# Four graph layers on one core: transfers of 125 rows issued as 112 and 13 rows, degrees in halves, weight sums earlier

## The chip, the core and the metric

The kernel runs on one core of a Trainium2 chip. The metric is the device time of one execution in microseconds: the median of the runs shown, beside the lowest and the highest. The core has five engines with instruction queues of their own, which wait for one another by semaphores: PE (matrix products, with PEld loading its weights), DVE (vector), ACT (scalar and table functions), POOL and SP. Here SP, ACT and POOL issue DMA transfers; 16 DMA engines move the data. The profile also names the clock that the throttle granted to PE: 1.00 is 2.4 GHz and 0.50 is 1.2 GHz.

## What is computed

x has 1250 nodes of 512 features, and 21250 directed edges (src, dst), own loops among them. Four graph layers follow one another, each as x = layernorm(x + layer(x)):

```
L0: h = x @ W_gat (8 heads of 64); alpha = softmax over the edges into a node of
    leaky_relu(a_src[src] + a_dst[dst]); out = sum of alpha * h[src]; batch norm, gelu, + x @ W_skip
L1: x0, x1 = linear(x); tpw = small network of 3 silu layers on edge_attr_8; per edge products of
    tpw, x[src] and edge_attr_4, summed by dst; linear; / 10
L2: s, t = (h @ W) @ a; att = softmax over the edges of leaky_relu(s[row] + t[col]);
    agg = sum of att * h[col]; out = silu(agg) @ base_w.T + sum over 8 B-splines basis(agg) @ spline_w
L3: neighbor_mean = sum over edges of x[src] / max(deg, 1); relu([x, neighbor_mean] @ w.T)
```

## The kernel before

Nodes lie as NB = 10 blocks of NP = 125 rows; edge lists lie as 125 rows of 170 edges. HB = 5 blocks are a half, KT = 4 blocks of 128 features make 512. Each engine's program is written out by hand, with its own order and constant semaphore counts; a DMA adds 16 to its semaphore when it has landed. The stages run in this order.

- **Start.** SP loads dst, src, edge_attr_4, edge_attr_8 and the second half of x (L539 to L543; 83, 83, 332, 664 and 1250 KB), ACT the first half of x and w_gat (L1420, L1421; 1250 and 1024 KB). DVE waits for dst (L1845) and sorts edges by destination; its first result (L1855) opens PE's stream: two small products, ten x_blocks of transposes (L838; the second half of x is awaited at L834), five gat_blocks (L845), then count_order (L819), which also needs DVE's second result (L1911). POOL scatters the sorted edge records to HBM (L717).
- **Counts and layer 0.** Edges become a 1250 x 1250 matrix of counts: cd (a view of cnt_d) and its transpose cnt_s. The edge network of layer 1 runs beside DVE's maxima; PE then waits for DVE at L1030. Eight attention heads follow.
- **Layer 1.** PE's linear_up makes xup; ACT copies each block to one of two buffers (L1663; from the third block on, it awaits the store of the block two before), SP stores it (L619), and POOL gathers the rows by edge after all ten (L774, L775).
- **Layer 2, attention.** In two halves: DVE makes row maxima (half_terms), PE and ACT spread them (half_rows), DVE makes tiles (half_tiles: t_tile L2067, ACT's exponential, p_tile L2071), PE multiplies x by them (L1261). DVE then adds the tiles (add_tile, L2294), reduces the degrees deg from cd (L2314), and waits for PE's column sums (L1271). rden2 = 1 / sums (L2319, L2322) scales feature blocks 0, 1, 2 of aggT (L2325), while PE still multiplies block 3 (L1290).
- **Spline stage.** 36 steps g (two halves of SUBS = 18): a function of aggT (silu for the first two steps of a half) from ACT and DVE, products with weight parts on PE (L1309 pairs, L1319 single). weight_sums(g) forms four sums of the loaded weight parts (L2331 to L2334; the first three are called at L2393, after the scaling), node_sums(g) four sums of the function's blocks (L2344 to L2347), which PE awaits. SP stores the counts to HBM (L641, 3052 KB) once rden2 is begun.
- **Layer 3.** PE makes z = x @ w_near (L1374); ACT copies the high part and stores it (L1802), DVE makes the low part and SP stores it (L668). POOL gathers a few rows of z after all twenty stores (L796 to L798), ACT copies them to big_z (L1829), and PE's gathered_part (L1400) uses them after near_part of block 0 (L1394) and self_part (L1384). SP stores the ten blocks of the output (L672) and waits for all.

Of the kernel before, what the change touches and what calls it, by code (L numbers as in the profile page):

```python
# [10 lines left out]
NP, NB = 125, 10  # L11
# [82 lines left out]
def build(nc, a, out):  # L94
# [8 lines left out]
    with ctx:  # L103
# [427 lines left out]

        def bass_row(v, p):
            return v.rearrange("(a n) -> a n", a=1).to_broadcast([p, v.shape[0]])
# [3 lines left out]
        def _(sp):  # L537

            sp.dma_start(dsti, a["dst"].rearrange("(p e) -> p e", p=NP)).then_inc(s_dst_in, 16)  # L539
            sp.dma_start(srci, a["src"].rearrange("(p e) -> p e", p=NP)).then_inc(s_rec_in, 16)  # L540
            sp.dma_start(a4, a["edge_attr_4"].rearrange("(p e) k -> p e k", p=NP)).then_inc(s_rec_in, 16)
            sp.dma_start(a8, a["edge_attr_8"].rearrange("(p e) k -> p e k", p=NP)).then_inc(s_rec_in, 16)
            sp.dma_start(x_sb[:, HB:, :], a["x"].rearrange("(b p) n -> p b n", p=NP)[:, HB:, :]).then_inc(s_x_in1, 16)  # L543
# [97 lines left out]
            sp.dma_start(cnt_rows.rearrange("(b p) n -> p b n", p=NP), cnt_s[:]).then_inc(s_cntrow_out, 16)  # L641
# [24 lines left out]
            for b in range(NB):  # L666
                sp.wait_ge(s_zlo_ok, b + 1)
                sp.dma_start(z_rows[N + b * NP:N + (b + 1) * NP, :], z_lo[:NP, b, :].bitcast(f32)).then_inc(s_zrow_out, 16)  # L668

            for b in range(NB):  # L670
                sp.wait_ge(s_x_ok, 3 * NB + b + 1)
                sp.dma_start(out[b * NP:(b + 1) * NP, :], x_sb[:, b, :]).then_inc(s_out_done, 16)  # L672
            sp.wait_ge(s_out_done, 16 * NB)
# [3 lines left out]
        def _(pool):  # L677
# [86 lines left out]
            def gathers(i, par, tiles):  # L764
# [8 lines left out]
                if par == 0:  # L773
                    pool.wait_ge(s_xup_out0, 16 * NB // 2)  # L774
                    pool.wait_ge(s_xup_out1, 16 * NB // 2)  # L775
# [16 lines left out]
            pool.wait_ge(s_cntrow_out, 16)  # L792
# [3 lines left out]
            pool.wait_ge(s_zrow_out, 16 * 2 * NB)  # L796
# [6 lines left out]
        def _(pe):  # L803
# [28 lines left out]
            def x_block(b):  # L832
                if b % HB == 0:
                    pe.wait_ge(s_x_in if b == 0 else s_x_in1, 16)  # L834
# [582 lines left out]
        def _(act):  # L1417
            A = nc.scalar.activation

            act.dma_start(x_sb[:, 0:HB, :], a["x"].rearrange("(b p) n -> p b n", p=NP)[:, 0:HB, :]).then_inc(s_x_in, 16)  # L1420
# [238 lines left out]
            def xup_out(b):  # L1659
                act.wait_ge(s_xup_ps, b + 1)  # L1660
                if b >= 2:
                    act.wait_ge(s_xup_out0 if b % 2 == 0 else s_xup_out1, 16 * (b // 2))
# [862 lines left out]
```

## Time and profile before

| | us |
|---|---|
| median of 3 runs (lowest, highest) | 1581.47 (1580.15, 1582.06) |
| profiled execution | 1582.99 |
| its span, first to last instruction | 1581.5 |
| busy in it: PE, DVE, ACT, POOL | 1373.6, 1354.2, 903.0, 480.1 |
| chain that ended last: PE, DVE, issue, ACT, DMA | 51%, 24%, 12%, 5%, 5% |
| mean granted clock of PE | 0.951 |

The chain is followed back from the last instruction, at each step to what released it. "issue" is time in which an engine waited for nothing that the profile shows. The DMA share is the mean busy share of the 16 DMA engines. In a row of the timeline the brackets hold the engine's idle time just before and what ended it.

### The profile page before, as it was taken

What the parts mean: (1) busy time and instruction counts of PE and PEld (TensorE: products, weight loads), DVE (VectorE), ACT (ScalarE), POOL (GpSimd) and SP (SyncE); (2) the same over time, 40 slices, a digit from 0 to 9 for tenths busy, and PEclk for the clock granted to TensorE, in tenths of its full rate; (3) what the DMA queues carried; (4) which work ended last, traced back from release to release, by engine and by line L of the source; (5) the groups of instructions that cost most, each with busy time, mean ns of one, the idle gap of its engine ahead of it and who ended that gap; (6) DMA issues with size and microseconds to landing.
All of it is one profiled execution on the core that took longest, in us unless ns stands there. A gap on an engine that the chain in (4) does not pass through costs nothing.

```text
span 1581.5 us, 25111 instructions
## 1 busy us (share of the span) xinstructions
PE 1373.6 (87%) x8237; PEld 885.5 (56%) x8237; DVE 1354.2 (86%) x2065; ACT 903.0 (57%) x1949; POOL 480.1 (30%) x488
## 2 busy tenths in 40 slices
PE   1978898837688887789999999979999999999997
PEld 1555444602333333566666666756667777776465
DVE  8875999899899999759999999777989979996244
ACT  1286555628565565558888888543168849772300
POOL 1788888840000100236666666200000000000000
PEclk9998999859899999689999999989999999999998
DMA  4201000126111210246666766400144444342301
GB/s 128 69 6 9 6 7 7 14 70 192 53 58 48 60 52 17 77 133 212 198 201 193 214 197 196 76 1 1 54 132 135 134 145 170 136 143 69 117 24 43
DMA packets 76686, 150.26 MB, mean 95 GB/s; under 512 B 13722, under 2 KB 32268, under 8 KB 76477
## 3 DMA queue, kind: packets, MB, share of 16 engines
q1 hardware_dynamic: 50531, 83.18, 16.1%
q0 software_dynamic: 23328, 59.50, 15.0%
q10 hardware_dynamic: 2746, 6.59, 1.3%
q8 instruction: 38, 0.62, 0.2%
q14 instruction: 43, 0.35, 0.1%
HBM read 116.13 MB, written 32.91 MB: 94 GB/s over the span
## 4 chain that ended last, share of the span: by engine, by line
PE 51%; DVE 24%; issue 12%; ACT 5%; DMA 5%; DVEq 2%; POOL 0%; SPq 0%; POOLq 0%; ACTq 0%
PE PS L1309 14%; DVE arena L2071 7%; DVE arena L2037 5%; PE PS L1167 5%; PE PS L1261 4%; PE PS L1319 4%; DVE arena L2067 3%; PE PS L931 3%; PE PS L1394 3%; PE PS L1153 3%; DVE arena L2233 3%; ACT arena L1456 2%; PE PS L845 2%; DMA x_sb<-in_x 2%; PE PS L1374 2%
## 5 line engine op out<-in xcount | busy, mean ns | idle before, releaser
L717 POOL DMA_INDIRECT recs<-arena x170 | 239.3, 1408 | 89.4 <-issue 88.8
L1079 PE MATMUL PS<-arena 125*128 125x512 f32 (+1 forms) x480 | 190.1, 533 | 43.4 <-DVE arena L2071 43.3
L781 POOL DMA_INDIRECT arena<-xup,gidx x205 | 194.8, 950 | 104.7 <-issue 52.4
L1167 PEld LDWEIGHTS PS<-arena 128*32 128x32 f32 x3280 | 174.1, 109 | 88.3 <-ACT arena L1694 81.9
L1694 ACT ACTIVATE arena<-arena,gslot 128x32 f32<-128x32 f32 x820 | 186.3, 309 | 55.2 <-PE PS L1167 48.0
L1167 PE MATMUL PS<-arena 128*32 128x128 f32 (+1 forms) x3280 | 201.9, 306 | 6.2 <-DVE arena L2225 3.9
L2225 DVE TENSOR_TENSOR arena<-PS,arena 128x1536 f32<-128x1536 f32 (+1 forms) x103 | 179.0, 1738 | 0.0
L1079 PEld LDWEIGHTS PS<-arena 125*128 125x128 f32 x480 | 85.6, 191 | 147.8 <-issue 77.6
L1626 ACT ACTIVATE arena<-arena,c 125x1250 f32<-125x1250 f32 x80 | 106.7, 1336 | 97.6 <-DVE arena L2067 97.6
L2067 DVE SCALAR_TENSOR_TENSOR arena<-arena,c 125x1250 f32<-125x1250 f32 (+1 forms) x100 | 137.7, 1380 | 14.0 <-ACT arena L1748 12.9
L1309 PE MATMUL PS<-arena,cnt_d 128*125 128x256 f32 x576 | 148.4, 380 | 0.0
L794 POOL DMA_INDIRECT cnt_d<-cnt_rows,bidx_c x1 | 0.9, 946 | 463.8 <-DVE bvalid L2453 463.8
L1309 PE MATMUL PS<-arena 128*125 128x256 f32 x432 | 118.1, 383 | 3.6 <-DVE cnt_d L2347 3.5
L1309 PEld LDWEIGHTS PS<-arena,cnt_d 128*125 128x125 f32 x576 | 108.7, 189 | 16.4
L1153 PE MATMUL PS<-arena 64*128 64x512 f32 x410 | 117.5, 649 | 0.0
L2071 DVE SCALAR_TENSOR_TENSOR arena<-arena,cnt_s 125x1250 f32<-125x1250 f32 x80 | 116.0, 1450 | 0.0
L1512 ACT ACTIVATE arena<-PS 125x626 uint16<-125x626 f32 x102 | 69.2, 692 | 60.1 <-PE PS L931 60.0
L1309 PEld LDWEIGHTS PS<-arena 128*125 128x125 f32 x432 | 81.6, 189 | 30.7 <-issue 20.2
L2221 DVE TENSOR_TENSOR arena<-PS,arena 128x512 f32<-128x512 f32 (+1 forms) x103 | 70.9, 688 | 19.4 <-DMA arena<-xup,gidx 14.8
L931 PE MATMUL PS<-arena 128*125 128x512 bf16 (+1 forms) x408 | 73.1, 311 | 15.8 <-DVE arena L1992 15.4
L2233 DVE TENSOR_TENSOR arena<-PS,arena 128x256 f32 x205 | 84.8, 414 | 1.3 <-PE PS L1167 0.5
L931 PEld LDWEIGHTS PS<-arena 128*125 128x125 bf16 x408 | 44.6, 142 | 63.7 <-DVE arena L1992 38.9
(395 smaller groups left out, 2536.2 us busy)
## 6 DMA issues: line engine op xcount, KB each, us to landing
arena<-in_spline_wT SPq DMA_DIRECT2D x32, 512.0 KB, 4.1
t_rows<-arena SPq DMA_DIRECT2D x18, 512.0 KB, 5.1
arena<-t_rows SPq DMA_DIRECT2D x18, 512.0 KB, 4.5
arena<-uv_rows SPq DMA_DIRECT2D x14, 610.4 KB
arena<-h_rows SPq DMA_DIRECT2D x26, 256.0 KB
h_rows<-arena SPq DMA_DIRECT2D x24, 256.0 KB, 2.8
arena<-xup,gidx POOLq DMA_INDIRECT x205, 3.7
cnt_rows<-cnt_s SPq DMA_DIRECT2D x1, 3051.8 KB
```

Of the source, the lines that this page charges most:

```text
L717: pool.indirect_dma_start(out=recs, out_offset=bass.IndirectOffsetOnAxis(pos[:, c:c + 1], 0), in_=rec[:, c, :], in_offset=None).then_inc(s ...
L781: pool.indirect_dma_start(out=ring[:, m, :], out_offset=None, in_=xup, in_offset=bass.IndirectOffsetOnAxis(gidx[:, par, m:m + 1], 0))\
L931: ins = t.matmul(PS[:NP, 2 * (n % 3) + q, 0:n1 - n0], oh_dst[:, n % (2 * WP), :, e], oh_src[:, 2 * (n % WP) + e, n0:n1], start=(e == 0), s ...
L1079: ins = t.matmul(PS[:, 3 * par + q, 0:n1 - n0], hs[:, sblk, par * C:par * C + 2 * C], wt[:, sblk % WR, n0:n1], start=(sblk == 0), stop=(sb ...
L1153: t.matmul(PS[:, tpw_bank[(2 * k + q) % 4], :], h3[r, buf, k * 128:(k + 1) * 128], w_m4[r, :], start=True, stop=True, tile_position=(q * H ...
L1167: ins = t.matmul(PS[quad * DB:(quad + 1) * DB, bank, o0 * MUL:o0 * MUL + w], sel4[:, s, v * DB:(v + 1) * DB], prod[:, s, c0 * MUL:c1 * MUL ...
L1309: ins = t.matmul(PS[:NP, bank, c * HD:(c + 1) * HD], lhs, w_part(g, w), start=(s == 0 and m in ((0, 1, 3, 6) if j == 0 else (0, 1, 3))), s ...
L1694: ins = A(sel4[:, s, y * DB:(y + 1) * DB], eq4[:, m // 4, s * DB:(s + 1) * DB], ACT.Copy, scale=gslot[:, par, c + R_Y + y:c + R_Y + y + 1])
L2067: v.scalar_tensor_tensor(dst, U, cc, V, ALU.add, ALU.max).then_inc(ok, 1)
L2071: v.scalar_tensor_tensor(dst, e, 1.0, cm, ALU.min, ALU.mult).then_inc(ok, 1)
L2225: v.tensor_tensor(pr[:, :, :, 1:4, :], w[:, :, :, 1, :].unsqueeze(3).to_broadcast([128, n, 2, 3, MUL]), xg[:, :, 1:4, :].unsqueeze(2).to_b ...
L2233: v.tensor_tensor(d, PS[:, 2 + m % 4, 0:256], d, ALU.add).then_inc(s_gsum_ok, 1)
```

## The change

Every transfer to or from 125 rows that SP and ACT issue, except recs, weights and rows of other shapes, is issued as two: rows 0 to 111 and rows 112 to 124. These are dst, src, both edge attributes and both halves of x, the xup blocks, the counts, the high and low z rows, and the output blocks. Their semaphore counts double. DVE's degree reduction is done by halves of five blocks: the first before the tiles of the first half of layer 2, the second where the whole was. The first three weight_sums move from behind the scaling of aggT to before the wait for the column sums. The scaling goes through blocks 0, 2, 1, and ACT's first silu, which uses blocks 0 and 2, waits for two blocks instead of three.

```
+        ROWS = (slice(0, NP // 16 * 16), slice(NP // 16 * 16, NP))
...
-            sp.dma_start(x_sb[:, HB:, :], a["x"].rearrange("(b p) n -> p b n", p=NP)[:, HB:, :]).then_inc(s_x_in1, 16)
+            for dst_tile, view, done in (
+                    (dsti, a["dst"].rearrange("(p e) -> p e", p=NP), s_dst_in),
...
+                    (x_sb[:, HB:, :], x_rows[:, HB:, :], s_x_in1)):
+                for r in ROWS:
+                    sp.dma_start(dst_tile[r], view[r]).then_inc(done, 16)
...
-                sp.dma_start(xup[b * NP:(b + 1) * NP, :], xup_st[:, b % 2, :]).then_inc(s_xup_out0 if b % 2 == 0 else s_xup_out1, 16)
+                for r in ROWS:
+                    sp.dma_start(xup[b * NP:(b + 1) * NP, :][r], xup_st[r, b % 2, :])\
+                      .then_inc(s_xup_out0 if b % 2 == 0 else s_xup_out1, 16)
...
-            sp.dma_start(cnt_rows.rearrange("(b p) n -> p b n", p=NP), cnt_s[:]).then_inc(s_cntrow_out, 16)
+            for r in ROWS:
+                sp.dma_start(cnt_rows.rearrange("(b p) n -> p b n", p=NP)[r], cnt_s[r]).then_inc(s_cntrow_out, 16)
...
+                for r in ROWS:
+                    sp.dma_start(z_rows[N + b * NP:N + (b + 1) * NP, :][r], z_lo[r, b, :].bitcast(f32)).then_inc(s_zrow_out, 16)
...
+                for r in ROWS:
+                    sp.dma_start(out[b * NP:(b + 1) * NP, :][r], x_sb[r, b, :]).then_inc(s_out_done, 16)
+            sp.wait_ge(s_out_done, 32 * NB)
...
+            for r in ROWS:
+                act.dma_start(x_sb[r, 0:HB, :], a["x"].rearrange("(b p) n -> p b n", p=NP)[r, 0:HB, :]).then_inc(s_x_in, 16)
...
-                    act.wait_ge(s_aggT_ok, KT + 1 if h else KT - 1 + s)
+                    act.wait_ge(s_aggT_ok, KT + 1 if h else KT if s else KT - 2)
...
+                for r in ROWS:
+                    act.dma_start(z_rows[b * NP:(b + 1) * NP, :][r], z_hi[r, b, :].bitcast(f32)).then_inc(s_zrow_out, 16)
...
+            def degrees(hf):
+                bs = slice(hf * HB, (hf + 1) * HB)
+                link(v.tensor_reduce(deg[:, bs], cd[:, bs, :], X, ALU.add))
+            degrees(0)
             half_tiles(0)
             half_terms(1)
             half_tiles(1)
             for j in range(1, NB):
                 add_tile(j)
-            link(v.tensor_reduce(deg[:], cd, X, ALU.add))
+            degrees(1)
...
+            for g in range(3):
+                weight_sums(g)
+
             dve.wait_ge(s_l2_agg, 3)
...
-            for f in range(KT - 1):
+            for f in (0, 2, 1):
                 dve.wait_ge(s_l2_cp, f + KT)
...
-            for g in range(3):
-                weight_sums(g)
             node_sums(0)
```

## Rows read from the trace of the kernel before

**Rows 1.** Stretches: busy us of each engine; granted clock, DMA share, GB/s.

```profile
14.00:27.00 13.00, 0.00 (x0) 0.00 (x0) 12.97 (x4) 0.00 (x0) 0.00 (x0) 1.00 0.32 128
38.00:44.00 6.00, 6.00 (x23) 4.51 (x24) 5.69 (x11) 2.95 (x5) 0.00 (x0) 1.00 0.87 294
```

**Rows 2.** Timeline of PE (start, us, engine, line, operation; idle before and its releaser).

```profile
38.00 4.64 PE L838 MATMUL PS<-ident,x_sb 125*128 125x125 f32 x20 [5.40 <-DMA x_sb<-in_x]
60.30 0.29 PE L819 MATMUL PS<-arena,upper 125*125 125x20 f32 x2
```

**Rows 3.** Timeline of POOL and DVE before the first PE work.

```profile
4.65 2.39 POOL L698 IOTA iota<- 128x416 f16 x1
5.45 1.69 DVE L1846 TENSOR_SCALAR arena<-arena 125x170 int32<-125x170 int32 x1 [3.03 <-DMA arena<-in_dst]
56.59 0.18 DVE L1911 TENSOR_TENSOR arena<-arena 125x19 f32<-125x19 f16 x1
```

**Rows 4.** Timeline of PE at the end of the small network.

```profile
400.72 4.56 PE L1030 MATMUL PS<-ident,uv 125*125 125x125 f32 x20 [8.54 <-DVEq L2057]
```

**Rows 5.** Chain (start, us, what) at xup; the page's DMA issues.

```profile
684.58 4.00 DMA xup<-arena
689.29 4.10 DMA xup<-arena
h_rows<-arena SPq DMA_DIRECT2D x24, 256.0 KB, 2.8
arena<-in_L_gnn_W_up SPq DMA_DIRECT2D x2, 64.0 KB, 1.9
```

**Rows 6.** Timeline of DVE and PE in layer 2, attention.

```profile
1062.29 1.65 DVE L2067 SCALAR_TENSOR_TENSOR arena<-arena,c 125x625 f32<-125x625 f32 x2 [2.87 <-ACT arena L1748]
1065.00 7.36 PE L1261 MATMUL PS<-arena,x_sb 125*128 125x512 f32 x14 [3.41 <-DVE arena L2071]
1125.11 13.17 DVE L2314 TENSOR_REDUCE deg<-cnt_d 125x10 f32<-125x12500 uint16 x1
1139.64 1.46 DVE L2319 TENSOR_SCALAR arena<-PS 128x1250 f32<-128x1250 f32 x1 [1.15 <-PE PS L1271]
```

**Rows 7.** Timeline, chain and one stretch at the start of the spline stage.

```profile
1139.36 16.97 PE L1290 MATMUL PS<-arena,x_sb 125*128 125x512 f32 x48
1149.13 4.20 DVE L2325 TENSOR_TENSOR arena<-arena 128x1250 f32<-128x1250 f32 x3
1157.67 0.42 DVE L2334 TENSOR_TENSOR arena<-arena 128x256 f32<-128x256 f32 x1
1159.81 1.88 PE L1309 MATMUL PS<-arena 128*125 128x256 f32 x4 [3.48 <-DVE cnt_d L2347]
...
1159.81 7.97 PE PS L1309 x28
1169.49 6.04 PE PS L1309 x28
1161.00:1162.00 1.00, 1.00 (x4) 0.76 (x3) 0.41 (x2) 1.00 (x2) 0.00 (x0) 0.50 0.97 322
```

**Rows 8.** Timeline of SP and PE, and the chain, at the z rows.

```profile
1464.12 24.64 SPq L668 DMA_DIRECT2D z_rows<-z_lo  x10
1484.25 14.90 DMA z_rows<-z_lo
1504.07 0.47 PE L1400 MATMUL PS<-big_z,big_cnt 128*125 128x512 f32 x1 [2.84 <-ACT big_z L1829]
1504.53 6.21 PE PS L1394 x20
1514.41 4.67 PE PS L1394 x20
```

**Rows 9.** Timeline of SP and its waits (us, times, longest), end.

```profile
1574.43 0.92 SPq L672 DMA_DIRECT2D out<-x_sb  x2
SPq L103 <- DMA out<-x_sb: 5.7, 1, 5.7
```

More of the change, by code:

```diff
@@ L537, in _ @@
         def _(sp):
[L539 to L542, printed above, removed]
-            sp.dma_start(x_sb[:, HB:, :], a["x"].rearrange("(b p) n -> p b n", p=NP)[:, HB:, :]).then_inc(s_x_in1, 16)
+            x_rows = a["x"].rearrange("(b p) n -> p b n", p=NP)
+            for dst_tile, view, done in (
+                    (dsti, a["dst"].rearrange("(p e) -> p e", p=NP), s_dst_in),
+                    (srci, a["src"].rearrange("(p e) -> p e", p=NP), s_rec_in),
+                    (a4, a["edge_attr_4"].rearrange("(p e) k -> p e k", p=NP), s_rec_in),
+                    (a8, a["edge_attr_8"].rearrange("(p e) k -> p e k", p=NP), s_rec_in),
+                    (x_sb[:, HB:, :], x_rows[:, HB:, :], s_x_in1)):
+                for r in ROWS:
+                    sp.dma_start(dst_tile[r], view[r]).then_inc(done, 16)
             sp.wait_ge(s_wdiag_zero, 1)
@@ L773, in gathers @@
                 if par == 0:
-                    pool.wait_ge(s_xup_out0, 16 * NB // 2)
-                    pool.wait_ge(s_xup_out1, 16 * NB // 2)
+                    pool.wait_ge(s_xup_out0, 32 * NB // 2)
+                    pool.wait_ge(s_xup_out1, 32 * NB // 2)
                 pool.nop(nofuse=True)
@@ L791, in _ @@
             pool.wait_ge(s_big_ok, 3)
-            pool.wait_ge(s_cntrow_out, 16)
+            pool.wait_ge(s_cntrow_out, 32)
             pool.nop(nofuse=True)
@@ L795, in _ @@
                                     in_offset=bass.IndirectOffsetOnAxis(bidx_c[:, 0:1], 0)).then_inc(s_bigrow_in, 16)
-            pool.wait_ge(s_zrow_out, 16 * 2 * NB)
+            pool.wait_ge(s_zrow_out, 32 * 2 * NB)
             pool.nop(nofuse=True)
@@ L833, in x_block @@
                 if b % HB == 0:
-                    pe.wait_ge(s_x_in if b == 0 else s_x_in1, 16)
+                    pe.wait_ge(s_x_in if b == 0 else s_x_in1, 32)
                 if b >= 2:
@@ L1661, in xup_out @@
                 if b >= 2:
-                    act.wait_ge(s_xup_out0 if b % 2 == 0 else s_xup_out1, 16 * (b // 2))
+                    act.wait_ge(s_xup_out0 if b % 2 == 0 else s_xup_out1, 32 * (b // 2))
                 A(xup_st[:, b % 2, :], PS[:NP, 2 + b % 2, :], ACT.Copy, scale=float(MUL) ** -0.5).then_inc(s_xup_cp, 1)
@@ L1801, in store_high @@
                 act.wait_ge(s_z_cp, b + 1)
-                act.dma_start(z_rows[b * NP:(b + 1) * NP, :], z_hi[:NP, b, :].bitcast(f32)).then_inc(s_zrow_out, 16)
+                for r in ROWS:
+                    act.dma_start(z_rows[b * NP:(b + 1) * NP, :][r], z_hi[r, b, :].bitcast(f32)).then_inc(s_zrow_out, 16)
             def x3_in(b):
@@ L1844, in _ @@
             v.memset(blk, 0.0)
-            dve.wait_ge(s_dst_in, 16)
+            dve.wait_ge(s_dst_in, 32)
             v.tensor_scalar(blk_i, dsti, DB.bit_length() - 1, None, ALU.arith_shift_right)
@@ L1855, in _ @@
             v.tensor_tensor(tot_e[:, 1:NDB], cum_e[:, 1:NDB, EC - 1], cum_e[:, 0:NDB - 1, EC - 1], ALU.subtract).then_inc(s_tot_ok, 1)
-            dve.wait_ge(s_rec_in, 48)
+            dve.wait_ge(s_rec_in, 96)
             v.tensor_scalar(rec[:, :, R_DL], dl_i, -1.0, None, ALU.mult)
@@ L2334, in weight_sums @@
                 v.tensor_tensor(t4, b21, t2w, ALU.subtract)
+            for g in range(3):
+                weight_sums(g)
+            dve.wait_ge(s_l2_agg, 3)
+            ins = v.tensor_scalar(rden2, PS[:, 0:3, :].rearrange("p a n -> p (a n)")[:, 0:N], 0.5, None, ALU.max)
+            ins.then_inc(s_psum_ok, 1)
+            dve.wait_ge(s_psum_ok, NB)
+            link(v.reciprocal(rden2, rden2))
+            for f in (0, 2, 1):
+                dve.wait_ge(s_l2_cp, f + KT)
+                v.tensor_tensor(aggT[:, f, :], aggT[:, f, :], rden2, ALU.mult).then_inc(s_aggT_ok, 1)
             def node_sums(g):
```

11 lines of the change are left out of this document (removed).

## The prediction

> **What bounds the kernel now.** I read the chain of work that ended last first, then the waits, then the timeline around each wait that a changed transfer or a moved step touches, and the table of stretches for the clock and the DMA share. The reader is to see that no single resource bounds the kernel: the stages follow one another, and a gain counts only where a wait of the chain's engine ends on what is changed. Four such waits are on transfers of 125 rows, and one is on DVE's order.
>
> The transfers themselves come first. In the stretch in which only 125-row loads run, the DMA share is 0.32 at 128 GB/s, which is 5 engines of 16; where 128-row transfers run it is 0.87 at 294 GB/s [rows 1]. So a 125-row transfer uses 5 engines. That 112 rows use 16 is likely from the 128-row rows, but no row shows 112 rows or 13.
>
> **Start (3.7 us gained).** PE transposes the first half of x, idles 5.40 us until the second half lands, and goes on at 38.00; it reaches the count products (L819) at 60.30 [rows 2]. DVE has what they need at 56.59 + 0.18 = 56.77 [rows 3], 3.53 us before. On 16 engines (294 GB/s, so 16 us for the 4.8 MB of all first loads) the second half is there long before 32.6, PE's idle time goes, and PE is 5.4 us early; but L819 then waits for DVE. So this place gives 3.53 us, plus what DVE itself gains. DVE starts at 5.45 when dst lands, 4.4 us after its issue. Its pieces should land at 3.4 (1.9 us, the 64 KB load [rows 5], after a second issue near 1.5) to 4.4. But L1846 lasts 1.69 us for 170 elements a partition, where L2314 reduces 12,500 in 13.17 [rows 6], 0.18 us for 170; and it ends just after POOL's iota, which ends at 4.65 + 2.39 = 7.04 [rows 3]. DVE was held by POOL, and an earlier dst would bring one or two short instructions ahead of that hold, not the rest. I take 0.2 us of the 2.0 possible: 3.7 in all, between 3.3 and 5.5. The Trainium skill, SBUF — State Buffer, "Who interferes with whom", says that DVE's two-port modes and a GpSimd instruction lock each other out for a whole instruction. The row agrees; without such a lock the whole kernel would come 1.2 us lower, at 1565.6.
>
> From L819 on everything hangs on DVE, PE and ACT in turn, so the 3.7 us travel. The one thing that doesn't move with them is POOL's scatter of records, which feeds the small network; that network ends early and PE then waits 8.54 us for DVE [rows 4], so it may fall behind by the 3.7 us.
>
> **xup rows (2.1 us gained).** A store takes 4.00 us, ACT refills the buffer, and the last store takes 4.10, after which POOL may gather [rows 5]. A 256 KB store from 128 rows lands in 2.8 us [rows 5]. The second piece is issued some 0.4 us after the first (two issues of SP take 0.92 us [rows 9]) and has little data; I take 3.0 us for a pair, between 2.8 and 3.6. That is 1.0 + 1.1 = 2.1 us, between 0.9 and 2.5.
>
> **Degrees, first half (3.8 us lost).** The reduction takes 13.17 us over ten blocks, so 6.6 for five. It is put before the tiles of the first half, where DVE idles only 2.87 us, from 1059.42 to 1062.29 [rows 6]. It ends near 1066.1, so the first tile is 3.8 us late, and PE waits for it already now (3.41 us before L1261 [rows 6]). Behind the tiles queue ACT's exponentials and PE's products. A block has twelve product entries of 7.36 / 14 = 0.53 us and only two DVE steps of 0.83 [rows 6], so DVE catches up and PE doesn't: 3.8 us, at most 4.2. If PE's clock rises sooner after the later restart, up to 1.9 us comes back (what a restart loses at rows 7).
>
> **Degrees, second half, and weight sums (hidden).** Now the reduction runs from 1125.11 to 1138.3, and DVE waits 1.15 us for PE's column sums [rows 6]. In its place come 6.6 us and the twelve weight sums, from the end of L2325 at 1153.3 to 1158.1, 4.8 us [rows 7]. They end near 1136.7, 2.9 us before PE's sums at 1139.6, and all of it moves by 3.8 together. Cover: PE's products up to the column sums. Without it each us would count.
>
> **Start of the spline stage (5.4 us gained).** Now DVE scales three blocks until 1153.3, does the weight sums, then the node sums, and PE starts L1309 at 1159.81 after waiting 3.48 us; its products of the stage before end at 1139.36 + 16.97 = 1156.33 [rows 7]. Without weight sums between, and with ACT's silu started after two of the three blocks, the node sums (1.7 us) end near 1155.0: PE is late next, with 1.3 us to spare. The 3.48 us go. PE also restarts at clock 0.50 (1.2 GHz), and its first 28 products take 7.97 us, against 6.04 later [rows 7]; without the idle time the clock stays at 2.4 GHz, another 1.93. Sum 5.4, at least 3.5 if the clock falls all the same. The moved block 1 is due only for the second silu, which waits for the fourth block anyway.
>
> **z rows (4.4 us gained).** After the last low block, the DMA backlog lasts 14.90 us from 1484.25; the gather and one ACT copy follow, and PE waits 2.84 us at L1400 [rows 8]. Its next products run slow after the idle time, 6.21 against 4.67 us [rows 8]: 2.84 + 1.54 = 4.4 us. In the new kernel the last pair lands 3.0 us after 1484.25, at 1487.3; the 4.9 us from landing (1499.15) to L1400 (1504.07) make 1492.2, and PE is ready at 1501.2. So 9 us of margin; at the least 2.8 us of the gain holds. ACT issues ten stores more, 0.26 to 0.4 us each, in blocks in which it waits for PE. The counts (3 MB, stored before the spline stage) have to land only before a gather far behind that stage, and on 16 engines they leave the weights' queue sooner.
>
> **Output (2.9 us gained).** SP issues the last two blocks in 0.92 us from 1574.43 and then waits 5.7 us, to 1581.05 [rows 9]. The last pair, issued near 1575.15, should land 3.0 us later, at 1578.15: 2.9 us, between 1.7 and 3.3.
>
> **Sum.** 3.7 + 2.1 - 3.8 + 5.4 + 4.4 + 2.9 = 14.7 us. The profiled execution took 1582.99 us, so 1568.3 by its own measure; the median of the runs shown is 1581.47, 1.52 lower, so the forecast is 1566.8. With all low ends, 3.3 + 0.9 - 4.2 + 3.5 + 2.8 + 1.7 = 8.0, it is 1573.5; with all high ends, 5.5 + 2.5 - 1.9 + 5.4 + 4.4 + 3.3 = 19.2, it is 1562.3.
>
> **Rivals.** (1) Early gains are absorbed: the 3.7 us of the start are lost in the record scatter or in POOL's locks. For: POOL's chain starts only 0.2 us earlier. Against: the 8.54 us [rows 4]. 1566.8 + 3.7 = 1570.5.
>
> (2) DVE's reorder gives nothing back: the node sums are not done by 1156.3 and the clock falls as now. For: only 1.3 us of margin. Against: every duration of that chain is in rows 7. 1566.8 + 5.4 = 1572.2.
>
> (3) The change doesn't spread: 112 rows run on few engines too. Then only 5.4 - 3.8 = 1.6 us are gained: 1579.9. For: no row has 112 rows. Against: the 5-engine rate for 125 = 25 x 5 and 16 engines for 128 look like shares of equal size, and 112 = 16 x 7.
>
> (4) Slower: the two pieces of a pair follow one another, each with its own landing. The z rows decide: 20 pieces on SP at (2.8 + 1.9) / 2 = 2.35 us each take 47 us from the first low store at 1464.1 [rows 8], so they land at 1511 where now they land at 1499.2, and L1400 is 12 us later; the output's four pieces take 9.4 us (+2.4), the two xup pairs 4.7 each (+1.3). Against 3.7 of the start and 1.6 of the reorder that makes 1581.5 + 15.7 - 5.3 = 1591.9. It turns the sign once a piece holds the queue for more than some 1.9 us. Against it: 125-row loads follow one another on one queue without a gap in the rate [rows 1]. The Trainium skill, SBUF — State Buffer, "Can I just issue two DMAs to hit both halves?", says that two transfers to different partitions serialize, and advises one transfer. Here the one transfer is on 5 engines, so the rule speaks against this change only if serializing includes the landing; the rate in rows 1 doesn't bear that out.
>
> **How the numbers follow.** Forecast (all terms within their bounds, 1562.3 to 1573.5) 0.70; rival 1 0.08 and rival 2 0.07, both inside that span; rival 3 0.07; rival 4 0.03; better than 1561.5, where something unseen is released, 0.05. The range 1561.5 to 1575 leaves out rivals 3 and 4 and the better case, and so holds 0.85. A measurement of this kernel can tell 0.2% (3.2 us) from no change: faster means below 1578.3. Faster 0.90; same 0.07 (rival 3); slower 0.03 (rival 4).
>
> **What would show it.** In the new profile: a DMA share well over 0.32 before 20 us and no idle time of PE before the second half of x, but a wait of some 1.9 us at L819 for DVE; xup stores near 3 us; PE's wait before the first L1261 grown from 3.4 to about 7.2 us; no wait and no half clock at the first L1309; no wait of PE on the gathered z; SP's last wait near 2.5 us. The prediction is wrong if stores of 112 rows still run near 128 GB/s, or if half the degrees finds more cover than 2.87 us.

## The result, and the profile after

The changed kernel takes 1569.62 us (median of 4 runs, 1569.24 to 1571.28), against 1580.81 for the kernel before in the same runs: a ratio of 0.9936, 95% interval 0.9921 to 0.9950. It is faster, by 11 us where 14.7 were forecast, and the time lies inside the range. Its profiled execution took 1571.28 us with a span of 1569.8; that of before took 1582.99 with 1581.5. So the two traces, which the readings below compare, are 11.7 us apart.

PE's products come in the same order in both kernels (the new lines stand 11 to 18 further down), so the start of one and the same product tells how far the new kernel is ahead at that place:

| product | before | after | ahead | gained since the row above |
|---|---|---|---|---|
| count products, L819 / L830 [rows 2] | 60.30 | 58.34 | 1.96 | 1.96 |
| first of the small network's end, L1030 / L1041 [rows 4] | 400.72 | 402.28 | -1.56 | -3.52 |
| second group of gathered edges, L1167 / L1178 | 706.94 | 702.96 | 3.98 | 5.54 |
| first attention products, L1261 / L1272 [rows 6] | 1065.00 | 1064.87 | 0.13 | -3.85 |
| second run of 28 spline products, L1309 / L1320 [rows 7] | 1169.49 | 1163.80 | 5.69 | 5.56 |
| z products after the wait for z_lo, L1374 / L1385 | 1464.14 | 1458.44 | 5.70 | 0.01 |
| second gathered part, L1400 / L1411 | 1510.58 | 1501.95 | 8.63 | 2.93 |
| end of the span | 1581.5 | 1569.8 | 11.7 | 3.07 |

Three rows of the kernel before that the table and the account of xup rest on (the first is from its chain, the others are from PE's timeline):

```profile
702.38 3.48 PE PS L1167 x24
1464.14 3.70 PE L1374 MATMUL PS<-arena 128*125 128x512 f32 x8 [1.65 <-DVE z_lo L2464]
1510.58 0.40 PE L1400 MATMUL PS<-big_z,big_cnt 128*125 128x512 f32 x1
```

Then stretches of the new kernel, with the columns of [rows 1]:

```profile
14.00:27.00 13.00, 0.00 (x0) 0.00 (x0) 13.00 (x1) 0.00 (x0) 0.00 (x0) 1.00 1.09 230
54.00:80.00 26.00, 21.37 (x71) 14.80 (x71) 22.43 (x34) 4.39 (x8) 22.34 (x13) 0.67 0.07 5
1459.00:1464.00 5.00, 5.00 (x12) 2.15 (x11) 1.78 (x3) 0.12 (x1) 0.52 (x1) 0.66 0.85 266
```

In the first row all 16 engines are busy (a share near 1), where before a share of 0.32 stood from 14 to 27 us [rows 1]. The last two tell of the clock: of the 26 us from 54 to 80, around and behind the count products, PE had (1 - 0.67) x 26 / 0.5 = 17.2 us at 0.50, and of 5 us in the z products, by the same working, 3.4.

Rows picked from its timeline:

```profile
8.47 0.25 DVE L1859 TENSOR_SCALAR arena<-arena 125x170 int32<-125x170 int32 x1 [6.04 <-DMA arena<-in_dst]
58.34 0.61 PE L830 MATMUL PS<-arena,upper 125*125 125x20 f32 x2 [3.94 <-DVE arena L1924]
402.28 4.56 PE L1041 MATMUL PS<-ident,uv 125*125 125x125 f32 x20 [8.62 <-DVEq L2070]
700.02 1.96 PE L1178 MATMUL PS<-arena 128*32 128x256 f32 x32 [1.07 <-DVE arena L2238]
702.96 1.95 PE L1178 MATMUL PS<-arena 128*32 128x256 f32 x32
1055.45 6.67 DVE L2324 TENSOR_REDUCE deg<-cnt_d 125x5 f32<-125x6250 uint16 x1
1062.16 1.65 DVE L2080 SCALAR_TENSOR_TENSOR arena<-arena,c 125x625 f32<-125x625 f32 x2
1064.87 15.33 PE L1272 MATMUL PS<-arena,x_sb 125*128 125x512 f32 x46 [7.28 <-DVE arena L2084]
1095.44 1.65 DVE L2080 SCALAR_TENSOR_TENSOR arena<-arena,c 125x625 f32<-125x625 f32 x2 [9.87 <-ACT arena L1760]
1136.15 0.42 DVE L2343 TENSOR_TENSOR arena<-arena 128x256 f32<-128x256 f32 x1
1139.26 1.46 DVE L2349 TENSOR_SCALAR arena<-PS 128x1250 f32<-128x1250 f32 x1 [2.69 <-PE PS L1282]
1155.87 1.03 PE L1320 MATMUL PS<-arena 128*125 128x256 f32 x4
1458.44 5.39 PE L1385 MATMUL PS<-arena 128*125 128x512 f32 x8 [1.65 <-DVE z_lo L2482]
1496.66 0.80 PE L1411 MATMUL PS<-big_z,big_cnt 128*125 128x512 f32 x1
1501.95 0.40 PE L1411 MATMUL PS<-big_z,big_cnt 128*125 128x512 f32 x1
```

Rows picked from the chain (start, us, what), then SP's wait at the end (total, times, longest):

```profile
1.51 6.94 DMA arena<-in_dst
684.72 0.30 SPq L626
685.07 2.60 DMA xup<-arena
1156.04 6.04 PE PS L1320 x28
1163.80 6.04 PE PS L1320 x28
```

```profile
SPq L103 <- DMA out<-x_sb: 1.9, 1, 1.9
```

The reader is to see five things. First, dst landed 6.94 us after its issue, at 8.45, and DVE's first instruction on it started at 8.47, not at 5.45 as in [rows 3]; it lasted 0.25 us, not 1.69. Second, PE waited 3.94 us for DVE before the count products and went on at half the clock. Third, a pair of xup stores takes 2.96 us from the end of ACT's copy to the landing (0.30 us of SP's issue of the second piece, 2.60 until that has landed, and the gaps between), where the one store took 4.0 by the same count. Fourth, the first degrees end at 1062.12, DVE's first tile starts right behind, and PE's wait before the attention products is 7.28 us, where it was 3.41 [rows 6]; at the spline stage, on the other hand, PE starts without a wait and its 28 products take 6.04 us. Fifth, no wait is left at the gathered z rows, and SP waits 1.9 us at the end, where it waited 5.7 [rows 9].

### The profile page after: what moved, and what is told of

The parts are those of the page before. It is cut to its first block, busy times and chain, and to the rows that moved or that the text cites. A ratio compares the mean times of both kernels' runs of the same rounds, so it can differ in the third digit from the quotient of the medians.

```text
span 1569.8 us, 25159 instructions
## 1 busy us (share of the span) xinstructions
PE 1370.8 (87%) x8237; PEld 884.0 (56%) x8237; DVE 1353.6 (86%) x2066; ACT 903.3 (58%) x1949; POOL 479.7 (31%) x488
## 4 chain that ended last, share of the span: by engine, by line
PE 45%; DVE 29%; issue 16%; ACT 5%; DVEq 3%; DMA 1%; POOL 0%; SPq 0%; POOLq 0%; ACTq 0%
PE PS L1320 14%; DVE arena L2084 7%; DVE arena L2050 5%; PE PS L1272 4%; DVE arena L2246 4%; PE PS L1330 4%; DVE arena L2080 3%; PE PS L1405 3%; PE PS L942 3%; ACT arena L1468 2%; PE PS L1385 2%; PE PS L1395 2%; DVEq L2246 2%; DVE arena L2005 2%; PE PS L1301 1%
## 5 line engine op out<-in xcount | busy, mean ns | idle before, releaser
L1178 PEld LDWEIGHTS PS<-arena 128*32 128x32 f32 x3280 | 173.1, 109 | 86.4 <-ACT arena L1706 79.8
L1178 PE MATMUL PS<-arena 128*32 128x128 f32 (+1 forms) x3280 | 200.4, 304 | 4.7 <-DVE arena L2238 2.2
L1320 PE MATMUL PS<-arena,cnt_d 128*125 128x256 f32 x576 | 147.8, 379 | 0.0
L1320 PEld LDWEIGHTS PS<-arena,cnt_d 128*125 128x125 f32 x576 | 108.1, 188 | 16.2
L1320 PE MATMUL PS<-arena 128*125 128x256 f32 x432 | 116.8, 379 | 0.1
L1320 PEld LDWEIGHTS PS<-arena 128*125 128x125 f32 x432 | 81.0, 188 | 26.6 <-issue 16.4
L942 PE MATMUL PS<-arena 128*125 128x512 bf16 (+1 forms) x408 | 73.5, 311 | 15.9 <-DVE arena L2005 15.5
```

The lines of the kernel that those rows point to most:

```text
L942: ins = t.matmul(PS[:NP, 2 * (n % 3) + q, 0:n1 - n0], oh_dst[:, n % (2 * WP), :, e], oh_src[:, 2 * (n % WP) + e, n0:n1], start=(e == 0), s ...
L1178: ins = t.matmul(PS[quad * DB:(quad + 1) * DB, bank, o0 * MUL:o0 * MUL + w], sel4[:, s, v * DB:(v + 1) * DB], prod[:, s, c0 * MUL:c1 * MUL ...
L1320: ins = t.matmul(PS[:NP, bank, c * HD:(c + 1) * HD], lhs, w_part(g, w), start=(s == 0 and m in ((0, 1, 3, 6) if j == 0 else (0, 1, 3))), s ...
```

## The experiments

Two theories stood after this first comparison. **S**: the start loses what it was to gain, because dst now shares the 16 engines with 4.7 MB of other loads and lands later, and PE's longer wait for DVE lowers its clock. **The rival**: the start did gain, and a later stage took it. Beside that, three terms of the sum were measured alone: the order of the degrees, the xup rows and the z rows. The kernel before took 1580.42 us beside the first four kernels, 1579.53 beside the next four and 1579.26 beside the last four; where two kernels ran beside different runs of it, their ratios to it compare better than their medians, and both are given where they differ. Readings of a few us rest on the traces.

**The changed kernel again.**

> The changed kernel itself, beside the variants of it. Every theory: 1569.6 us, within 1. Theory S (the start lost what it was to gain: dst lands 3.0 us later because all first loads now share the 16 engines, DVE ends its count 1.5 us later, and PE, which waits 3.94 us for it, goes on at a granted clock of 0.50) expects dst to land near 8.4 us again, PE's wait before the count products near 3.9 us and a stretch at 0.50 after it in this execution too. Theory R (the low clock of that stretch belongs to the one execution) expects the clock at 1.00 from 60 to 67 us in this one.

Measured: 1571.68 us (1567.57 to 1574.63), ratio 0.9938 (0.9923 to 0.9953), 2.1 us above the first four executions. In its trace DVE starts on dst at 8.02, PE waits 3.53 us before the count products, and the granted clock from 54 to 80 us is 0.80, which is 10.4 us at 0.50. So the wait and the low clock belong to the kernel, but how long the clock stays low differs from one execution to the next.

**First loads whole.**

```
...
-                for r in ROWS:
-                    sp.dma_start(dst_tile[r], view[r]).then_inc(done, 16)
+            sp.dma_start(dsti, a["dst"].rearrange("(p e) -> p e", p=NP)).then_inc(s_dst_in, 16)
...
```

> The changed kernel with the first loads (dst, src, both edge attributes, both halves of x) in one transfer each, as before; xup, counts, z rows, output and DVE's order stay changed. Theory S (the start lost): dst lands near 5.4 us, the count products start at 60.3 us without a wait before them, and the time is 1.6 us under the changed kernel, where the trace of the changed kernel stands behind the one of before at 400 us: 1568.0, down to 1566.2 if the 3.4 us by which it stands behind at 70 us are lost for good. Rival A (the start did gain its 3.7 us and a later stage takes them, the records' scatter or the small network): 3.7 us slower where they are felt, 1573.3, or no change, 1569.6, where all are absorbed.

Measured: 1568.9 us (1566.27 to 1569.36), ratio 0.9921 (0.9908 to 0.9933). Timeline of DVE and PE, and the stretch after the count products:

```profile
5.54 1.60 DVE L1854 TENSOR_SCALAR arena<-arena 125x170 int32<-125x170 int32 x1 [3.12 <-DMA arena<-in_dst]
59.82 0.29 PE L826 MATMUL PS<-arena,upper 125*125 125x20 f32 x2
```

```profile
54.00:80.00 26.00, 24.52 (x94) 13.48 (x93) 20.61 (x34) 5.58 (x12) 22.00 (x14) 0.93 0.08 6
```

dst lands at 5.5 us again, DVE is held for 1.60 us, PE reaches the count products without a wait, and from 54 to 80 us the clock is low for 3.6 us, as in the kernel before (0.93 there as well). The kernel is not slower than the changed one, so the rival falls: no later stage was living on a gain of the start. How large the loss is, the traces say better than two medians 0.7 to 2.8 us apart. Seven executions have the split start and the same code up to the small network's end (the changed kernel twice, and five kernels below); PE starts there at 402.28, 402.19, 401.35, 401.00, 400.50, 399.96 and 399.85, 401.0 on the mean. Before and with whole loads it is 400.72 and 400.28. So the split start is worth 400.5 - 401.0 = -0.5 us, between -1.8 and 0.7, and not 3.7; the profiled execution of the changed kernel was the slowest of the seven.

**First half of the degrees later.**

```
-            degrees(0)
             half_tiles(0)
             half_terms(1)
+            degrees(0)
             half_tiles(1)
```

> The changed kernel with the first half of the degrees moved from ahead of the tiles of the first half to ahead of the tiles of the second half, where DVE idles 9.87 us and the reduction takes 6.67. Theory D (the first half costs its whole overhang, since PE waits for DVE's first tile): PE's products of that stage start 3.9 us sooner, nothing behind moves, 3.9 us gained: 1565.7. Rival B (something else holds PE there, or the second tile stage becomes late): 1569.6 or above.

Measured: 1565.3 us (1560.95 to 1565.71), ratio 0.9897 (0.9884 to 0.9910). Rows picked from the timeline of DVE and PE at the two halves:

```profile
1060.12 27.28 PE L1272 MATMUL PS<-arena,x_sb 125*128 125x512 f32 x96 [3.41 <-DVE arena L2084]
1080.97 6.67 DVE L2324 TENSOR_REDUCE deg<-cnt_d 125x5 f32<-125x6250 uint16 x1 [0.15 <-DVE uv L2297]
1089.39 1.65 DVE L2080 SCALAR_TENSOR_TENSOR arena<-arena,c 125x625 f32<-125x625 f32 x2 [1.75 <-ACT arena L1760]
```

PE's wait is back at 3.41 us. The same 6.67 us of reduction now stand where DVE idled 9.87 us (1095.44 in the new kernel's timeline), of which 1.75 are left. Theory D holds: 3.9 us of PE's wait lay in the place alone. The whole gain is larger than that: 4.3 us against the first median of the changed kernel, 6.2 by the two ratios, and in the traces 5.2 us from PE's products of L1207 to the second run of 28 spline products (117.0 us here, 122.3 in the changed kernel). Behind the shorter wait PE's clock was back at 1.00 after 3.1 us, behind the longer one after 5.9; no run tells why. The kernels below are built on this one, except the next.

**DVE's order of before, transfers split.**

```
-            degrees(0)
             half_tiles(0)
...
-            degrees(1)
+            link(v.tensor_reduce(deg[:], cd, X, ALU.add))
...
+            for g in range(3):
+                weight_sums(g)
             node_sums(0)
```

> The changed kernel with DVE's order of before (degrees whole behind the tiles' sums, weight sums behind the scaling, scaling 0, 1, 2, silu after three blocks); all transfers stay split. If the terms read from the two traces hold (degrees 3.9 us lost, spline start 5.5 gained), it is 1.6 us slower than the changed kernel: 1571.2. Rival C (the reorder gives nothing back at the spline start, and that gain in the trace is the transfers'): 3.9 us faster, 1565.7.

Measured: 1569.83 us (1565.96 to 1574.35), ratio 0.9931 (0.9914 to 0.9948). The medians don't separate 1569.8 from the changed kernel's 1569.6 and 1571.7. Timeline of PE at the first spline products, and two stretches:

```profile
1154.90 2.04 PE L1320 MATMUL PS<-arena 128*125 128x256 f32 x4 [3.48 <-DVE cnt_d L2360]
```

```profile
1154.00:1159.00 5.00, 4.10 (x11) 3.38 (x12) 3.74 (x8) 3.46 (x3) 0.00 (x0) 0.66 0.28 108
1459.00:1464.00 5.00, 4.80 (x14) 2.36 (x15) 2.97 (x6) 1.18 (x3) 0.95 (x1) 1.00 0.71 219
```

The wait of 3.48 us and the low clock are back exactly as in [rows 7], so the spline gain belongs to DVE's order, and rival C falls. The second stretch shows something else: here the same place in the z products, behind the same wait for z_lo, runs at 1.00, where the changed kernel had 0.66.

**dst ahead of all other loads.**

```
                 for r in ROWS:
                     sp.dma_start(dst_tile[r], view[r]).then_inc(done, 16)
+                if done is s_dst_in:
+                    sp.wait_ge(s_dst_in, 32)
...
+            act.wait_ge(s_dst_in, 32)
             for r in ROWS:
...
```

> The variant with the later first half of the degrees (1565.3), in which SP and ACT also hold all loads behind dst until dst has landed. Theory S1 (dst lands late because the other first loads share the 16 engines with it): dst lands near 3.5 to 4 us instead of 8.4; its first instruction on DVE lasts until POOL's 2.39 us instruction ends at 7.04, so the first product starts at 26.3 to 27.2 instead of 27.8 to 28.7, PE's wait before the count products shrinks by as much, and the gain is 0.6 to 1.5 us: 1564.3. Rival S2 (the 13-row piece lands late by itself): dst lands near 8 us all the same, and everything is later by the held loads or equal, 1565.3 or more.

Measured: 1562.97 us (1561.89 to 1567.91), ratio 0.9901 (0.9879 to 0.9922). Timeline of DVE and POOL:

```profile
3.28 3.86 DVE L1862 TENSOR_SCALAR arena<-arena 125x170 int32<-125x170 int32 x1 [0.85 <-DMA arena<-in_dst]
3.31 1.18 POOL L709 IOTA iota_src<- 128x1250 f16 x1
4.64 2.39 POOL L711 IOTA iota<- 128x416 f16 x1
```

S1 holds: left alone, the same two pieces land before 3.28 us. And the instruction that then starts lasts 3.86 us instead of 0.25: it ends at 7.14, with POOL's second long instruction (4.64 + 2.39 = 7.03). The hold by POOL, which the prediction read from 1.69 us, is here seen at its full length. The first product starts at 27.13, 0.67 us before the kernel this one is built on; the medians are 2.3 us apart, which is more than the start explains, but by the ratios (0.9901 and 0.9897) nothing is gained. The Trainium skill, DMA: Bandwidth & Descriptors, "Queues, rings and completion order", says that a DMA engine takes turns between its queues, a packet at a time; the late landing of dst beside other loads (8.45 us, and 3.28 without them) agrees with it. But this run holds back both ACT's loads and those behind dst on SP's own queue, so how much of the delay comes from either isn't shown.

**POOL's two long instructions first, as well.**

```
...
+            pool.iota(iota2[:].rearrange("p (c t) -> p c t", t=2), pattern=[[1, NT], [0, 2]], base=0, channel_multiplier=0,
+                      allow_small_or_imprecise_dtypes=True)
+            pool.iota(iota_src[:], pattern=[[1, N]], base=0, channel_multiplier=0, allow_small_or_imprecise_dtypes=True)
             pool.memset(upper[:], 1.0)
...
```

> As the variant before it (loads held until dst has landed), and POOL's two longest instructions of the start (1.18 and 2.39 us) moved to the head of its list. Theory L (the first instruction on dst is held by POOL, not by dst itself): it lasts 0.25 us and starts near 3.6 to 4, the first product starts near 23.5, 4.3 us before that of the variant without it, and the count products near 53: 3 to 4.4 us gained against 1565.3, so 1561.5. Rival (the 1.69 us belong to the first instruction on a fresh transfer, or PE becomes the bound at its start): the first product starts near 25 or PE is late by the 1 to 2 us between, 1563 to 1564.

Measured: 1563.05 us (1559.65 to 1564.40), ratio 0.9892 (0.9872 to 0.9912). Timeline of DVE and POOL:

```profile
3.22 0.42 DVE L1862 TENSOR_SCALAR arena<-arena 125x170 int32<-125x170 int32 x1 [0.80 <-DMA arena<-in_dst]
3.52 1.21 POOL L693 IOTA iota_src<- 128x1250 f16 x1
3.57 1.26 DVE L1863 TENSOR_SCALAR arena<-arena 125x170 int32<-125x170 int32 x1
```

The first instruction on dst takes 0.42 us at 3.22, so the hold is POOL's and no price of a fresh transfer. But the hold moved: the next instruction lasts 1.26 us, to the end of POOL's other long one (3.52 + 1.21 = 4.73). The first product starts at 25.50, 1.6 us sooner than with dst first alone, not 3.6. In its trace PE ends the small network's wait 2.2 us sooner (398.43 and 400.62 us); in the median nothing of it is seen.

**PE kept at work until the count products.**

```
-                for k in range(KT):
+                for k in tuple(range(KT)) * (2 if done is s_h_ps and b == HB - 1 else 1):
...
```

> The variant with the later first half of the degrees (1565.3), with the products of one block done a second time with the same result, 3.47 us of idle work on PE, so that PE runs on to within 0.5 us of the count products instead of waiting 3.9 us for DVE. Theory C (the wait is what lowers the clock): no stretch at 0.50 from 57 to 67 us, the products behind start 2.5 us or more sooner at 68 us than in the variant without it, and 1 to 2.5 us are left of that at 400 us: 1563.5. Rival (the clock falls there in any case, or the filler only takes time): the stretch at 0.50 is there again, 1565.3 or above.

Measured: 1561.98 us (1558.97 to 1564.73), ratio 0.9890 (0.9869 to 0.9911). Timeline and stretch (the kernel it is built on has a clock of 0.67 in that stretch, like the changed kernel above):

```profile
57.08 0.39 PE L830 MATMUL PS<-arena,upper 125*125 125x20 f32 x2
```

```profile
54.00:80.00 26.00, 21.76 (x87) 11.96 (x85) 20.76 (x34) 7.63 (x20) 22.04 (x14) 0.93 0.08 5
```

There is no wait, and the clock is low for 3.6 us instead of 17.2. These 3.6 us begin at 64.3, so the expectation of none before 67 was not quite met; the kernel before has them too, from 67.7, behind the same later products. A filler of 3.4 us (20.77 us for six blocks' products, where five took 17.33) makes everything behind 5.5 us sooner: the first of L902's products starts at 76.45 instead of 81.94, and the second gathered part, near the end, at 1490.35 instead of 1495.81. The medians show 3.3 and the ratios 1.1. That PE gains by products that serve nothing shows that it is the wait that lowers the clock: theory C holds, but its size is known only between these figures.

**Real work in PE's wait.**

```
-            for b in range(HB):
+            for b in range(HB + 1):
                 gat_block(b)
             count_order()
...
-            gat_block(HB)
```

> The variant with the later first half of the degrees (1565.3), with one block's products (3.47 us, which PE does now after the count products, on the path to ACT's scaling of the lanes) moved into PE's 3.9 us wait ahead of them. Theory C (clock) and the moved work together: no stretch at 0.50 from 57 to 67 us and 3.4 us less ahead of ACT's first scaling, whose data DVE has ready near 72: 3.4 plus 1 to 2.5 us, 1560 near. Rival (only the work moves, the clock falls anyway): 1561.9. Rival (DVE sets that place): 1565.3.

Measured: 1558.02 us (1556.37 to 1559.95), ratio 0.9862 (0.9839 to 0.9884). Timeline of PE:

```profile
57.81 0.39 PE L830 MATMUL PS<-arena,upper 125*125 125x20 f32 x2 [0.46 <-DVE arena L1923]
```

The wait is 0.46 us, and the clock stays at 1.00 until 64.3 us. It is then low for 6.8 us; the mean of 0.83 from 54 to 80 us counts 2.1 us more, from a stretch that begins at 77.9 in a later wait of 3.44 us for ACT and that lies behind 80 us in the kernels without this move. 7.3 us are gained on 1565.3 by the medians, 5.5 by the ratios and 5.9 in the traces (the second gathered part at 1489.87), where clock and moved work together were put at 4.4 to 5.9. The idle filler alone gave 5.5 in the traces, so most of this gain may be the clock; by the medians the two kernels are 4.0 us apart, and how much the moved work adds stays open.

**Output blocks in different pieces.**

```
...
+                cuts = ((125,), (120, 125), (112, 125), (96, 125), (64, 125),
+                        (80, 125), (128 - 16, 120, 125), (124, 125), (112, 125), (64, 112, 125))[b]
+                for r0, r1 in zip((0,) + cuts, cuts):
+                    sp.dma_start(out[b * NP + r0:b * NP + r1, :], x_sb[r0:r1, b, :]).then_inc(s_out_done, 16)
...
```

> The variant with the later first half of the degrees, whose ten output blocks are stored in different pieces: 125; 120+5; 112+13; 96+29; 64+61; 80+45; 112+8+5; 124+1; 112+13; 64+48+13 rows. Each block but the last stands alone in its 4.9 to 8.5 us, so the stretch of its data and the DMA share in it show how many engines it had. Theory N (a piece runs on the largest number of engines up to 16 that divides its rows, as 125 on 5 and 128 on 16): 125 rows at a share near 0.31 for some 2 us; 120 rows on 15 engines, 112, 96, 80 and 64 on 16, all near 0.9 for some 0.7 us; 124 rows on 4 engines (0.25, longer than 125 whole); the small pieces 5, 13, 29, 61 and 45 on few engines, 29 and 61 on one, so 64+61 would be no faster than 125 whole. Rival T (only whole multiples of 16 spread): 120 rows run at 0.31 or below like 125. Rival U (any piece below 125 spreads evenly): 124 and 61 near 0.9 too.

Measured: 1565.13 us, one execution. Stretches of the stores' data, in order 125; 120+5; 112+13; 64 and then 61; 124+1 rows (the last two columns are the DMA share and GB/s):

```profile
1500.70:1503.50 2.80, 2.80 (x14) 2.22 (x13) 0.00 (x0) 0.00 (x0) 0.00 (x0) 1.00 0.33 97
1509.10:1510.40 1.30, 1.30 (x7) 1.05 (x6) 0.00 (x0) 0.00 (x0) 0.00 (x0) 1.00 0.74 197
1517.40:1518.50 1.10, 1.10 (x6) 0.89 (x5) 0.00 (x0) 0.00 (x0) 0.00 (x0) 1.00 0.77 233
1534.40:1535.00 0.60, 0.60 (x5) 0.47 (x4) 0.00 (x0) 0.00 (x0) 0.00 (x0) 1.00 0.86 191
1535.00:1541.00 6.00, 6.00 (x21) 3.56 (x20) 3.12 (x7) 0.12 (x1) 0.00 (x0) 1.00 0.08 24
1555.40:1559.60 4.20, 0.32 (x2) 0.00 (x0) 3.66 (x8) 0.29 (x1) 0.00 (x0) 0.83 0.23 63
```

A share of 0.0625 is one engine of 16. 125 rows run on 5 engines for 2.80 us, 112+13 on nearly all for 1.10; 96 and 64 rows start near 0.86 (0.85 for the 96, in 0.80 us), but the 29 and 61 rows behind them are left to one engine (0.07 and 0.08) for 3.0 and 6.0 us; 124 rows run on 4 (0.23). So 64+61 takes 6.6 us, over twice the whole block. Theory N holds, T and U fall. The Trainium skill, DMA: Bandwidth & Descriptors, "Why a DMA increments its semaphore by 16 and not by 1", has the rule: the number of engines is the largest one up to 16 that divides the slowest dimension of both sides, which is the rows here. The trace agrees for 125, 124, 96, 64, 61 and 29 rows; the pieces of 5, 13 and 45 rows don't stand alone in it.

**Later degrees, block in the wait, dst first and POOL's order together.**

> The later first half of the degrees, the block moved into PE's wait (these two 1558.0), loads held until dst has landed and POOL's two long instructions first. If they add up, DVE's count ends 2.3 us sooner and PE, which starts sooner too, does the moved block by then: 1558.0 - 2 = 1556, between 1554.5 and 1557. Rival (PE's own work up to the count products, 29.7 us from its first product, is now late by more than DVE, or another wait takes the rest): 1558.

Measured: 1555.35 us (1553.95 to 1560.01), ratio 0.9846 (0.9820 to 0.9872). The count products start 2.6 us sooner than with the block alone:

```profile
55.19 0.39 PE L832 MATMUL PS<-arena,upper 125*125 125x20 f32 x2 [0.73 <-DVE arena L1926]
```

PE still waits 0.73 us there. The clock stays at 1.00 until 60.2 us, 5.0 behind the wait, and is then low for 10.2 us; no run tells what did that. (The mean of 0.75 from 54 to 80 us counts 2.7 us of the later wait for ACT as well.) The kernel beats the one before by 24 us and the changed one by 14.

**xup rows whole.**

```
-                for r in ROWS:
-                    sp.dma_start(xup[b * NP:(b + 1) * NP, :][r], xup_st[r, b % 2, :])\
...
+                sp.dma_start(xup[b * NP:(b + 1) * NP, :], xup_st[:, b % 2, :]).then_inc(s_xup_out0 if b % 2 == 0 else s_xup_out1, 16)
```

> The variant with the later first half of the degrees (1565.3), with the xup blocks stored in one transfer each, as before. The prediction's 2.1 us for xup: 1567.4. The trace of the changed kernel (products over the last two blocks 1.2 us sooner, first gathered edges another 1.2, and 1.6 us of products that no longer run at 0.50): 4 us, 1569.3. Rival (the later edge loop waits for something else anyway): 1565.3.

Measured: 1569.05 us (1568.24 to 1569.37), ratio 0.9928 (0.9902 to 0.9953), 3.75 us above the kernel it is built on (4.9 by the ratios). The chain, then PE's first gathered products here and in the kernel it is built on:

```profile
684.29 3.94 DMA xup<-arena
688.94 4.09 DMA xup<-arena
```

```profile
702.02 3.52 PE L1176 MATMUL PS<-arena 128*32 128x256 f32 x32 [2.73 <-DVE arena L2236]
```

```profile
697.77 3.64 PE L1178 MATMUL PS<-arena 128*32 128x256 f32 x32 [0.96 <-DVE arena L2238]
```

Both stores are back at 4 us. In the changed kernel the first gathered products ran at the higher clock (1.96 us), but not in the kernel that this one is built on (3.64 us, and 3.31 to 3.42 with whole loads or DVE's order of before), so a faster clock there isn't what the split rows bring. What they bring is steady: from PE's last products before the stores (L1113 of the kernel before) to the second group of gathered edges it takes 21.4 and 21.3 us in the two profiled kernels with whole xup rows, 17.2 in the changed kernel, 17.7 in the one that this is built on, and 15.9 to 17.9 in all twelve with split rows.

**z rows whole.**

```
-                for r in ROWS:
-                    sp.dma_start(z_rows[N + b * NP:N + (b + 1) * NP, :][r], z_lo[r, b, :].bitcast(f32)).then_inc(s_zrow_out, 16)
+                sp.dma_start(z_rows[N + b * NP:N + (b + 1) * NP, :], z_lo[:NP, b, :].bitcast(f32)).then_inc(s_zrow_out, 16)
...
```

> The variant with the later first half of the degrees (1565.3), with the high and low z rows stored in one transfer each, as before. If the prediction's term holds (2.84 us of wait for the gathered rows and 1.54 at the lower clock behind it): 1569.7. Rival (a stretch at 0.50 near 1452 us belongs to the split stores, and is gone with them): 3.0 us, 1568.3. Rival (other traffic was the cause, the counts that are now off the queue): the z rows land in time even whole, 1565.3.

Measured: 1565.51 us (1564.35 to 1572.88), ratio 0.9927 (0.9898 to 0.9955): 0.2 us above its base by the medians and 4.7 by the ratios, so the times don't settle it. SP's stores, the last landing in the chain, and PE:

```profile
1450.86 22.28 SPq L677 DMA_DIRECT2D z_rows<-z_lo  x10
```

```profile
1472.68 13.09 DMA z_rows<-z_lo
```

```profile
1490.98 0.47 PE L1410 MATMUL PS<-big_z,big_cnt 128*125 128x512 f32 x1 [1.32 <-ACT big_z L1840]
```

The wait is back, but 1.32 us long and not 2.84. From the first low store to the last landing the DMA takes the same time in both: 1450.86 to 1485.77, 34.9 us, and 35.0 in [rows 8]. What differs is PE: here its clock fell behind the wait for z_lo, and it needs 38.8 us to where it could use the gathered rows (1450.88 to 1490.98 - 1.32); before, at full clock, 37.1 (1464.14 to 1504.07 - 2.84). The slower PE covers part of the wait. As this kernel has that low stretch too, it doesn't belong to the split stores. In its trace the whole stores cost 1.6 us from there to the second gathered part (45.06 us, and 43.50 in the kernel it is built on).

## Why the prediction was right, and where its terms were off

**Spreading** was right, and with it the rejection of rivals 3 and 4: the 112 rows run on all engines, and the small piece does not wait for the landing of the large one.

**Start: forecast 3.7, measured -0.5 (-1.6 in the profiled execution).** The step that failed is "its pieces should land at 3.4 to 4.4". It took the landing of a small load from the row of a 64 KB load at another place of the kernel [rows 5]. The same paragraph spread all first loads over 16 engines, so dst had to share each engine with x; it landed at 8.45, past the end of POOL's hold at 7.04, and DVE came 1.5 us late instead of 0.2 early. Alone it landed by 3.28. The second omission: the paragraph saw that L819 would wait for DVE, and priced the wait at nothing, since DVE sets the pace. Through the clock the wait costs 5.5 us by itself in the pair of traces with and without filler, 3.3 between their medians and 1.1 by their ratios. The hold by POOL was read rightly. Rival 1 named a loss of the same 3.7 us (1570.5), but as one taken later by the scatter or POOL; the loss is at the start itself.

**xup: forecast 2.1, measured 3.75 by the medians (in the traces 4.1 between before and after, 3.6 between the kernels with and without the split alone).** The mechanism is right, and in the profiled execution so is the price of a pair, 2.96 us where 3.0 was put. The sum was too small: it added two shorter stores and nothing behind them. In the profiled pair the first gathered products also ran at the higher clock (1.96 us, 3.48 before). In the kernel with the later degrees they didn't, and there the waits shrank by more instead: PE's next products start 2.17 us after its last ones before the stores and the gathered ones 10.89 us after that, where it is 3.68 and 13.05 with whole rows. So the size is shown, and its make-up differs from one execution to the next.

**Degrees, first half: forecast -3.8, measured -3.85** in the table; when it was moved 4.3 us came back by the medians and 5.2 in the traces, the wait and some clock behind it. **Second half and weight sums: hidden**, as forecast: the last weight sum ends at 1136.57 and DVE waits 2.69 us for PE, 2.9 were forecast. **Spline start: forecast 5.4, measured 5.56**, with wait and clock as they were costed; without the new order both are back, so rival 2 falls too.

**z rows: forecast 4.4, measured 2.93.** The wait of 2.84 us and the slow products behind it are gone as forecast, and in the execution with whole loads 4.63 us are gained over the same two rows of the table (41.81 us, 46.44 before). But in the profiled execution of the changed kernel PE's clock was at 0.50 for 3.41 us near 1460, behind the wait of 1.65 us for z_lo, which stands in both kernels. It makes the products of this row 1.7 us longer (5.39, 3.70 before). Of the fourteen profiled executions the clock fell there in nine. In the kernel before and four others it did not, behind the same wait. What decides is open; the length of the wait doesn't, and neither do the split stores. With whole stores that loss is partly covered, with split ones it counts: the split is worth 4.6 us where the stretch is in neither execution, and 1.6 where it is in both.

**Output: forecast 2.9, measured 3.07** between the two traces; no run changes the output alone back.

Measured, the terms make -0.5 + 3.75 - 3.85 + 5.56 + 2.93 + 3.07 = 11.0, against 11.2 between the medians. That the sum closes so well says little, since its terms come from different pairs of runs. And that the time falls only 2.8 us above the forecast is in part luck: the start missed by 4.2 us and the z rows by 1.5, and 1.65 us more than forecast at xup made up for a part of it. In the profiled pair the start lost 1.56 by 400 us, and PE was back at -0.31 (667.96 and 668.27) before the xup stores; stretches at 0.50 differ between the two traces there, and no run tells why. One price of the rivals is off: in rival 4 the output's four pieces, 9.4 us against the 6.6 of [rows 9], make 2.8 us more and not 2.4; nothing hangs on it.

## What to carry to other kernels

A transfer's rows decide how many engines it gets, so cut it where the large piece has 16 as a divisor and the rest has a large one too, or is short: the small piece is to be looked at as well as the large one. Once loads spread over all engines they also meet there: the one load that opens the work has to go first, and what waits for the others has to be looked up again. A wait of PE that "costs nothing" since another engine sets the pace is to be checked for the granted clock of the products behind it; moving real work into it was worth 5.5 to 7.3 us here, as much as the largest part of the change (5.56 at the spline stage).

## What the hardware showed

- A DVE instruction of 0.25 us lasted 3.86 when it started beside two of POOL's (1.18 and 2.39 us), and ended with them.
- A load of 83 KB landed at 5.45 us on 5 engines and at 7.1 to 8.5 on 16 with the other loads beside it; with those held back it was there by 3.3.
- In nine executions PE waited 3.5 to 4.2 us before the count products, and its clock fell to 0.50 in that wait or at most 1.0 us behind it. In five it waited 0.73 us or less, and the clock stayed at 1.00 for 5 us or more behind it.
- 61 rows took 6.0 us on one engine, longer than 125 rows on five (2.80).
